# Splitting the fourth column group of P as well, its low half by a subtraction on TensorE and a ScalarE copy

## The reference, cut to what matters

```python
Wh = x @ W                                      # x: 4096 x 256 after a layer norm
e = leaky_relu(e_src[:, None] + e_dst[None, :], 0.2)
e = where((adj > 0) | eye, e, -9e15)            # adj: 4096 x 4096
alpha = softmax(e, axis=1)
x = x + alpha @ Wh                              # the attention stage
x = x + ffn(layernorm(x))                       # router, top 2 of 8 experts, two products
```

## Time and profile before

| what | value |
|---|---|
| median of three runs | 993.97 us |
| the profiled execution | 993.66 us |
| its span, from first to last instruction | 991.9 us |
| TensorE busy | 948.2 us, 96% |
| VectorE busy | 790.4 us, 80% |
| ScalarE busy | 613.7 us, 62% |
| GpSimd busy | 635.0 us, 64% |
| granted TensorE clock | 0.995 |

### The profile page before, as it was taken

One profiled execution on the slowest core, in us unless ns is written; L12 is line 12 of the kernel. 1 busy time (PEld: TensorE's weight loads), 2 busy tenths in 40 slices (PEclk: granted clock), 3 DMA queues, 4 the chain that ended last, 5 costly groups with the idle time before them and its releaser, 6 DMA issues. The chain is left out here.

```text
span 991.9 us, 22957 instructions
## 1 busy us (share of the span) xinstructions
PE 948.2 (96%) x7550; PEld 797.4 (80%) x7551; DVE 790.4 (80%) x1210; ACT 613.7 (62%) x900; POOL 635.0 (64%) x632
## 2 busy tenths in 40 slices
PE   4999999999999999999999999999999999999994
PEld 3888999889988898889888977777777777777762
DVE  7689998999999999999999446787666676577653
ACT  3789898878888887878786544334333433333441
POOL 5312251295875865847729458888888888888652
PEclk9999999999999999999999999999999999999998
DMA  8548879787888697886877986443332332232321
GB/s 276 98 160 233 294 230 273 220 234 251 249 247 294 184 296 227 251 248 196 262 252 202 360 340 205 92 111 60 60 55 44 49 58 43 43 54 42 45 34 22
DMA packets 92236, 170.97 MB, mean 172 GB/s; under 512 B 19952, under 2 KB 69360, under 8 KB 83824
## 3 DMA queue, kind: packets, MB, share of 16 engines
q1 hardware_dynamic: 58384, 134.07, 40.4%
q0 software_dynamic: 24048, 26.23, 16.9%
q10 hardware_dynamic: 9712, 9.45, 3.4%
HBM read 136.91 MB, written 41.19 MB: 180 GB/s over the span
## 5 line engine op out<-in xcount | busy, mean ns | idle before, releaser
L1130 ACT ACTIVATE hf<-tp,b_cols 128x256 f32<-128x256 f32 (+1 forms) x312 | 116.2, 459 | 177.0 <-PE tp L882 174.3
L774 PE MATMUL acc<-wh,pt_hi 128*128 128x256 f16 x768 | 209.4, 273 | 0.0
L775 PE MATMUL acc<-wh,pt_hi 128*128 128x256 f16 x768 | 209.4, 273 | 0.0
L776 PE MATMUL acc<-wh,pt_lo 128*128 128x256 f16 x768 | 209.4, 273 | 0.0
L552 POOL TENSOR_TENSOR x_late<-x_late,wsp 128x1024 f32<-128x1024 f32 x32 | 78.8, 2463 | 170.0 <-DMA x_late<-in_L_ffn_W 164.9
L898 PE MATMUL acc<-w_sb,h_hi 128*128 x568 | 171.1, 379 | 5.3 <-issue 3.9
L1279 DVE SCALAR_TENSOR_TENSOR sc<-t_row,s_col 128x2048 f32<-128x2048 f32 x64 | 162.6, 2541 | 8.6 <-PE tp L755 6.7
L658 POOL DMA_INDIRECT out<-y_sb,yidx x71 | 121.7, 1714 | 66.7 <-DVE y_sb L1602 39.6
L880 PE MATMUL tp<-x_hi,w_sb 128*128 128x256 f16 (+1 forms) x624 | 161.3, 264 | 1.9 <-ACT hf L1130 1.8
L882 PE MATMUL tp<-x_down,w_sb 128*128 128x256 f16 (+1 forms) x624 | 161.4, 264 | 0.0
L881 PE MATMUL tp<-x_lo,w_sb 128*128 128x256 f16 (+1 forms) x624 | 161.0, 263 | 0.0
(11 more groups left out here) (240 smaller groups left out, 1787.8 us busy)
## 6 DMA issues: line engine op xcount, KB each, us to landing
adj_sb<-in_adj SPq DMA_DIRECT2D x64, 1024.0 KB, 7.4
x_late<-in_L_ffn_W SPq DMA_DIRECT2D x32, 512.0 KB, 9.8
wsplit_dram<-wsp SPq DMA_DIRECT2D x32, 512.0 KB, 8.9
w_sb<-wsplit_dram SPq DMA_DIRECT2D x32, 512.0 KB, 8.9
xs<-rows_dram ACTq DMA_DIRECT2D x32, 260.0 KB, 3.4
wsp<-in_L_ffn_W POOLq DMA_DIRECT2D x32, 256.0 KB, 4.8
x<-in_x SPq DMA_DIRECT2D x32, 128.0 KB, 9.6
out<-x SPq DMA_DIRECT2D x32, 128.0 KB
```

Source lines behind the costliest of these rows:

```text
L774: pe.matmul(o, pt_hi[g][:, cols], wh[:, j, 0, :], start=(j == 0), stop=False)
L775: pe.matmul(o, pt_hi[g][:, cols], wh[:, j, 1, :], start=False, stop=False)
L776: m = pe.matmul(o, pt_lo[g][:, cols], wh[:, j, 0, :], start=False, stop=False)
```

## The change

- Group 3 is split as the others are: H3 writes f16 into `pt_hi[3]`. `wh` now holds all 32 tiles in high and low halves, so `wh32` and `pt32` are gone and A3 is 24 f16 matmuls.
- The low half of group 3 isn't made by VectorE. A new piece on TensorE, here called S (`subtract_high`), waits for H3 and adds two matmuls onto the transposed values still in `tp[1]`: the stationary operand is `minus`, an identity times -1/1024, the moving one is 512 columns of `pt_hi[3]` each. What remains in the bank is P less its high half. A new piece on ScalarE, here called R (`p_rest`), waits for S and copies the bank as f16 into `pt_lo[3]`.
- TensorE's order becomes T0, A2 of i-1, T1, A3 of i-1, T2, A0, T3, A1, S. T1 and A3 wait for R of tile i-1, S waits for H3.
- ScalarE's order becomes R of i-1, H0, first mask half, H1, exps, and so on as before.
- The transposes are written as matmuls with `is_transpose`, so that for group 3 only the first of each bank clears it.
- The four pairs that were in `wh32` get a `wh_lo` on VectorE. `wh_lo(4)` and `wh_lo(5)` come after `wh_lo(3)`; `wh_lo(10)` and `wh_lo(11)` come after `masked(1, 1)`. The waits for them grow with it, and `project(14)` now waits for `wh_lo(10)`.
- GpSimd makes `minus`, one more constant ahead of TensorE's start.

```diff
         def p_transpose(i, u, g):
                 if g == 1 and i > 0:
-                    pe.wait_ge(s_hi, G * i)
+                    pe.wait_ge(s_lq, i)
...
+            def subtract_high(i):
+                pe.wait_ge(s_hi, G * i + G)
+                for h in range(2):
+                    cols = slice(h * GW // 2, (h + 1) * GW // 2)
+                    m = pe.matmul(tp[1][:, cols], minus[:, :], pt_hi[GS][:, cols], start=False, stop=True, skip_group_check=True)
+                m.then_inc(s_sub, 1)
...
                     p_transpose(i, u, 0)
...
+                if i > 0:
+                    av(i - 1, 1 - u, 2)
+                if now:
                     p_transpose(i, u, 1)
                 if i > 0:
-                    av(i - 1, 1 - u, 2)
                     av(i - 1, 1 - u, 3)
...
                     av(i, u, 1)
+                    subtract_high(i)
...
+            def p_rest(i):
+                act.wait_ge(s_sub, i + 1)
+                if within(i, 1, T):
+                    act.wait_ge(s_av, G * i)
+                act.activation(pt_lo[GS][:, :], tp[1][:, :], ACT.Copy, scale=PSCALE).then_inc(s_lq, 1)
...
+                if i > 0:
+                    p_rest(i - 1)
                 if now:
                     p_hi(i, 0)
...
                 if ahead:
                     mask(i + 2, u, 0)
+                if now:
+                    p_hi(i, 1)
```

More of the change, by code:

```diff
@@ L123, in build @@
         sc = [sb(f"sc{u}", [P, N], F32, front) for u in range(2)]
[L124 to L128, removed]
+        wh = sb("wh", [P, T, 2, D], F16, front)
+        pt_hi = [sb(f"pt_hi{g}", [P, GW], F16, front) for g in range(G)]
+        pt_lo = [sb(f"pt_lo{g}", [P, GW], F16, front) for g in range(G)]
         x_late = sb("x_late", [P, N], F32, front)
@@ L160, in build @@
         off_diag = sb("off_diag", [P, P], BF16, front)
+        minus = sb("minus", [P, P], F16, front)
         lg = sb("lg", [P, RB, E], F32, front)
@@ L180, in build @@
         xnt_pair += [wsp[1 + p // 2][:, (p % 2) * 4 * D:(p % 2 + 1) * 4 * D].bitcast(F32) for p in range(6)]
-        xnt_pair += [b[:, :].bitcast(F32) for b in pt_hi + pt_lo]
+        xnt_pair += [b[:, :].bitcast(F32) for b in pt_hi[0:GS] + pt_lo[0:GS]]
         late_pairs = [0, 1, 2, 3, 12, 13, 10, 11, 4, 5, 14, 15, 6, 7, 8, 9]
-        lows = [p < 2 * TS // 4 for p in late_pairs]
         side = (xt_ps, rt_ps)
@@ L265, in build @@
         s_lo = sem("p_lo_done")
+        s_sub = sem("p_high_subtracted")
+        s_lq = sem("p_lo_by_act_done")
         s_av = sem("av_done")
@@ L513, in _ @@
                       allow_small_or_imprecise_dtypes=True).then_inc(s_pc, 1)
+            pool.wait_ge(s_pc, 1)
+            pool.tensor_scalar(minus[:, :], ident[:, :], -1.0 / PSCALE, 0.0, ALU.mult, ALU.add).then_inc(s_pc, 1)
             def scales(m):
@@ L687, in _ @@
         def _(pe):
-            pe.wait_ge(s_pc, 8)
+            pe.wait_ge(s_pc, 9)
             def pair_t(p):
@@ L722, in project @@
                     pe.wait_ge(s_whh, max(2, 2 * (j - 3)))
-                    pe.wait_ge(s_whl, max(2, 2 * sum(lows[:j - 3])))
+                    pe.wait_ge(s_whl, max(2, 2 * (j - 3)))
                 for h in range(2):
@@ L747, in p_transpose @@
                 if g == 1 and i > 0:
[L748 removed]
+                    pe.wait_ge(s_lq, i)
                 if g == 1 and i == 0:
[L750 removed]
+                    pe.wait_ge(s_whl, T - 2)
                     pe.wait_ge(s_whh, T - 2)
@@ L754, in p_transpose @@
                 for c in range(GJ):
-                    m = pe.transpose(tp[g % 2][:, c * P:(c + 1) * P], sc[u][:, (GJ * g + c) * P:(GJ * g + c + 1) * P], ident[:, :])
+                    m = pe.matmul(tp[g % 2][:, c * P:(c + 1) * P], sc[u][:, (GJ * g + c) * P:(GJ * g + c + 1) * P], ident[:, :],
+                                  is_transpose=True, start=(g < GS or c % (GJ // 2) == 0), stop=True, skip_group_check=True)
                 m.then_inc(s_t, 1)
@@ L763, in av @@
                 else:
-                    pe.wait_ge(s_hi, G * i + G)
+                    pe.wait_ge(s_lq, i + 1)
                 if g == 0 and within(i, 2, T):
@@ L767, in av @@
                 if g == 1 and i == 0:
-                    pe.wait_ge(s_whl, TS)
+                    pe.wait_ge(s_whl, T)
                     pe.wait_ge(s_whh, T)
@@ L772, in av @@
                     cols = slice(c * P, (c + 1) * P)
[L773 to L778, removed]
-                m.then_inc(s_av, 1)
+                    pe.matmul(o, pt_hi[g][:, cols], wh[:, j, 0, :], start=(j == 0), stop=False)
+                    pe.matmul(o, pt_hi[g][:, cols], wh[:, j, 1, :], start=False, stop=False)
+                    m = pe.matmul(o, pt_lo[g][:, cols], wh[:, j, 0, :], start=False, stop=(j == T - 1))
+                m.then_inc(s_av, 1)
+            def subtract_high(i):
[4 more added lines that the diff above has]
+                m.then_inc(s_sub, 1)
             def router_t(b, h):
@@ L837, in attend @@
                     av(i, u, 1)
+                    subtract_high(i)
                 if in_batch(b) and q == 2:
                     router_mm(b, 1)
-            pe.wait_ge(s_whl, 2 * sum(lows[:NP - 2]))
+            pe.wait_ge(s_whl, T - 4)
             pe.wait_ge(s_whh, T - 4)
@@ L959, in wh_of @@
             def wh_of(n):
-                return wh32[:, n - TS:n - TS + 2, :] if n >= TS else wh[:, n:n + 2, 0, :]
+                return wh[:, n:n + 2, 0, :]
             def wh_hi(j):
@@ L995, in p_hi @@
                     act.wait_ge(s_av, G * i + g - 3)
-                dst = pt_hi[g] if g < GS else pt32
-                act.activation(dst[:, :], tp[g % 2][:, :], ACT.Copy, scale=PSCALE).then_inc(s_hi, 1)
+                act.activation(pt_hi[g][:, :], tp[g % 2][:, :], ACT.Copy, scale=PSCALE).then_inc(s_hi, 1)
+            def p_rest(i):
[3 more added lines that the diff above has]
+                act.activation(pt_lo[GS][:, :], tp[1][:, :], ACT.Copy, scale=PSCALE).then_inc(s_lq, 1)
             def normalise(b, k):
@@ L1060, in attend @@
                 ahead = i + 2 < T
+                if i > 0:
+                    p_rest(i - 1)
                 if now:
                     p_hi(i, 0)
-                    if i == 0:
-                        wh_hi(NP - 1)
+                if i == 0:
+                    wh_hi(NP - 1)
                     p_hi(i, 1)
-                if i == 0:
                     first_step()
@@ L1106, in _ @@
                 attend(i)
+            p_rest(T - 1)
             def expert_of(t):
@@ L1474, in _ @@
             wh_lo(3)
+            wh_lo(4)
+            wh_lo(5)
             wh_lo(6)
@@ L1482, in _ @@
             masked(1, 1)
-            for j in range(12, NP - 1):
+            for j in range(10, NP - 1):
                 wh_lo(j)
```

1 line of the change is left out of this document (removed).

## The result

The changed kernel takes 1008.95 us, median of four runs (1005.1 to 1010.25), against 994.38 for the kernel before on the same chip (993.95 to 996.27): a ratio of 1.0134 [1.0101, 1.0167]. It is slower, as forecast, by 14.6 us where 9 were forecast. Its profiled execution took 1005.1 us with a span of 1003.2, 11.3 us over the span before; that is the one to hold against the sum. (In the experiments, three executions of other kernels came out one and a quarter to two and a half times as long as their neighbours; they are left out.)

A forecast was written before the change was run, and what follows sets the result against it. TensorE seemed the bound, with the new ring through ScalarE, H3 and S deciding; run-up 3.3, blocks 6.9 and tail -0.9 gave +9.3 us on 993.66, so 1003 (chance 0.70, own range 997 to 1009), given range 992 to 1011.

The forecast's parts named there:

- The plain ring: Plain tile, from one S through ScalarE and H3 to the next S: 14.71 us instead of 14.81, TensorE waiting 0.3.
- The normalising tile: Tile where ScalarE also does four normalise copies: 16.74 us instead of 14.81, TensorE waiting 2.3 for H3.
- The routing tile: Tile where TensorE also does the routers' work: 17.06 us instead of 18.20, so 1.14 less.
- The run-up: Before tile 0 and through the first tiles: T0 of tile 0 1.4 us later, T0 of tile 3 3.4 later.
- first rival: TensorE's saving comes through, each tile 0.42 us shorter: 980 us, or 987 with half the ScalarE charge regained; chance 0.13.
- The third: S runs at the f32 pace, 0.86 us instead of 0.43: 13.8 us more, 1017; chance 0.06 together with the fourth.
- the fourth: Adding onto the transposed bank needs extra instructions, looking like the third in time; chance 0.06 together with the third.
- The second: A draw at 993 us, within 0.3%: VectorE has 62 us of work in a block of 64.3; chance 0.11.
- The blocks: Groups of four tiles from tile 4 to tile 30, summed against the kernel before: +6.9 us in all.
- the one-hot tile 19: Tile where TensorE waits in `router_pos` for the one-hots, 6.39 us after L1 starts: 16.4 us against 16.47.
- The tail: From T0 of tile 31 to the expert stage: two shorter A3, less one S and 0.3 of waiting, -0.9 us.
- VectorE has 8% left.: Attention stage: VectorE busy 469.3 of 511.9 us, read as 8% left, with TensorE at 501.0 seeming the bound.

The follow-up runs named there:

- T1 in the middle of A2: The changed kernel with T1 moved between the two halves of A2 on TensorE: 1004.41 us, ratio 1.0083.
- S twice: The changed kernel with the subtraction made in two passes of half the weight, four matmuls instead of two, same result: 1022.12 us, ratio 1.0272.
- the changed kernel's copy: The changed kernel run again unedited, beside three later experiments: 1006.16 us, ratio 1.0124.
- T1 in the middle and the copies spread: The changed kernel with T1 between the halves of A2 and four normalise copies spread over normalising and routing tiles: 996.95 us, ratio 1.0015.

## Why the prediction was right, and where its sizes were off

Right, by its steps (predicted, then measured in the profiled execution):

- A3 2.62 and 2.62; S 0.43 and 0.43 to 0.45; TensorE's own work in a plain tile 14.39 and 14.40 (T1 in the middle of A2).
- The plain ring 14.71 and 14.71 to 14.72, with a wait of 0.3 ahead of S. By the issue gap of the Trainium skill ("TensorE: Matmul & The Clock Gate", Back-to-back issue gap) S would have been 0.26 (and this ring 14.54, not below 14.5 as the prediction has it); S twice added 0.43 to it, so the row it was taken from held.
- The normalising tile 16.74 and 16.67 to 17.4, with the wait of 2.3 for H3 at 2.1 to 2.3; VectorE's L2 waits 1.55 there (over 1.4 was said). The routing tile 17.06 and 16.93 to 17.28, but for the two with a fallen clock (18.6).
- R: 0.92 from its start to the next copy's (337.06 to 337.98) and 1.02 long, not 1.15. The Trainium skill ("ScalarE: Activation LUTs", What ACT_TABLE_LOAD costs) has a second figure, 186 ns plus 0.833 ns per element for an ACTIVATE with immediate scale and bias, and 93 ns of overlap in a row. From it I estimate 1.04 and 0.95. That is the one to use for R, whose scale is an immediate, and the rows agree with it within 0.03; the figure that the prediction took is given there for a bias that is a pointer operand, which R hasn't.
- The run-up: T0 of tile 0 1.1 us later (1.4 was said), T0 of tile 3 3.2 (3.4). T1 of tile 1 waits 1.60 for R. In the profile of the changed kernel's copy the two are 2.4 and 4.5 later, so this part varies by over 1 us from one execution to the next.

Of the first rival (TensorE's saving comes through, 980) little is left: with T1 in the middle and the copies spread, the kernel still isn't faster than before. The third (S at the f32 pace) and the fourth are answered by S's 0.44 us. The second, a draw, is where the kernel goes once the ring is mended. It came true of that kernel, not of this one.

Off were three sizes:

1. *The missing term is TensorE's clock.* The prediction took the clock as full throughout, as the earlier trace rows show it. With the added waits came stretches of 3.4 us at 1.2 GHz, 1.7 us each. The profiled execution has two, both behind waits of over 2 us: 3.3 of its 11.3 us. That the waits bring them is argued from all the profiles, not shown by a run of its own. Its mean clock is 0.994, that of the other three runs 0.991 to 0.992, and these are 3 to 5 us longer; this is most of why the median is 1009 and not 1005. That each further loss is such a stretch was seen only in profiled executions, not in those three.
2. *The blocks.* Without the clock they gave +5.8 where 6.9 was said (T0 to T0: tiles 4 to 7 +1.2 for 2.2, then +2.5, +0.6, +1.3, +0.7, -0.7, +0.2 for 0.6, 1.5, 0.6, 1.4, 0.7, -0.1). Single blocks miss by up to 1.9, in both directions; two of the causes were traced, both on VectorE. In tile 9 its masked starts 1.75 us after T0, not 0.8 as in tile 17, so the exps start later and the tile has 17.43. In the one-hot tile 19 the step from L1 (376.12) to the one-hots (383.39) is 7.27 instead of 6.39, 0.9 more, and the tile 17.26 instead of 16.4: one instruction on the way takes 1.97 us where it took 1.15 before, and 0.15 where GpSimd leaves it alone, as the rows at the end show. The tail gave -0.7 for -0.9. So 3.1 + 5.8 + 3.3 - 0.7 = 11.5 at the end of the stage's products, and 11.3 in the span.
3. *"VectorE has 8% left."* True over the stage, and misleading. Within a block VectorE works 61.9 us of 64.3, and its rests sit where it waits for others (1.36 us for H2 in tile 17, behind the same four normalise copies). With half of A3 left out the block didn't get shorter. Nor are the 61.9 all work: in tiles 16 to 19 of the kernel before some 3.8 us of them, an estimate, are VectorE held up beside GpSimd (two scores halves of 4.32 and 3.18 instead of 2.34, and 1.15 instead of 0.15; see the end). The second rival had this reason (62 us of work in a block of 64.3); the first rival's 980 took for granted that TensorE's savings are worth their length. They weren't, and it should have had less than 0.13.

Open: whether the change pays if VectorE is relieved first, for instance with S and R for a second group in place of its L, or with GpSimd's `TENSOR_TENSOR` of L553 moved out of its way; neither was tried.

## What to carry to other kernels

When work moves to an engine with a small share, follow its order round the ring to the next tile: here 0.92 us on an engine at 62% cost nothing by itself, while one wait moved ahead of the bound's whole next tile cost 2 us every fourth tile. A saving on the busiest engine is worth at most the distance to the second busiest within the same block, and here it was worth nothing there; measure this first by leaving some of the work out. An engine's busy time can hold time in which another engine holds it up, so compare the lengths of equal instructions before taking it for work. Where waits of about 2 us are new on TensorE, allow for the clock as well, and move the work that causes them rather than the work that shows them: spreading four small copies gave back more than any change to the new pieces.

## What the runs showed of the hardware that was not expected

- In an otherwise full stage TensorE's granted clock fell to 1.2 GHz for 3.4 us (once 6.8) around the end of waits of 1.69 to 3.57 us, 27 times in the attention stages of eleven profiles, and nowhere else in them. It didn't fall behind all of them: two of the seven waits of 2.1 to 2.3 us for H3 in the changed kernel's profile. In the one profile with these waits filled with useless matmuls it didn't fall in the attention.
- The way from ScalarE through S and back, the end of H3 (353.03) to the start of R (353.73), is 0.70 us, of which 0.61 is S itself: by this trace the two handovers between these engines cost less than 0.1 us together. The ends of matmuls are modelled, so the split is rough; the 0.70 isn't.
- VectorE and GpSimd hold each other up. Some VectorE instructions take longer beside GpSimd's `TENSOR_TENSOR` of L553. The timeline of VectorE in the changed kernel, tiles 7 and 17 to 19, then that of GpSimd:

```profile
186.26 0.15 DVE L1380 TENSOR_TENSOR gap_l<-top 128x4 f32<-128x4 f32 x1
...
344.35 2.34 DVE L1298 SCALAR_TENSOR_TENSOR sc<-t_row,s_col 128x2048 f32<-128x2048 f32 x1
...
350.46 4.12 DVE L1298 SCALAR_TENSOR_TENSOR sc<-t_row,s_col 128x2048 f32<-128x2048 f32 x1
...
361.57 2.34 DVE L1298 SCALAR_TENSOR_TENSOR sc<-t_row,s_col 128x2048 f32<-128x2048 f32 x1
...
380.73 1.97 DVE L1380 TENSOR_TENSOR gap_l<-top 128x4 f32<-128x4 f32 x1
```

```profile
350.28 2.15 POOL L553 TENSOR_TENSOR x_late<-x_late,wsp 128x1024 f32<-128x1024 f32 x1
...
363.41 2.50 POOL L553 TENSOR_TENSOR x_late<-x_late,wsp 128x1024 f32<-128x1024 f32 x1 [3.26 <-DMA x_late<-in_L_ffn_W]
...
380.56 2.12 POOL L553 TENSOR_TENSOR x_late<-x_late,wsp 128x1024 f32<-128x1024 f32 x1 [10.57 <-DMA x_late<-in_L_ffn_W]
```

A scores half by itself has 2.34 us (344.35). The one at 350.46 begins 0.18 us after GpSimd's instruction and has 4.12. The one at 361.57 is under way when GpSimd's begins; it keeps its 2.34, and GpSimd's takes 2.50 instead of some 2.13. The instruction of 128 x 4 has 0.15 us by itself (186.26); the one at 380.73 lasts until 382.70, 0.02 us longer than GpSimd's.

The eleven profiles repeat this. Of their 704 scores halves 111 took over 2.45 us, all of them beside that `TENSOR_TENSOR`; in 87 GpSimd's had begun first, in 23 more it began less than 0.2 us later. Where it began later than that beside a half of usual length, GpSimd's took up to 4.1 us, longer by about what was left of the half. L0 to L2, which read one operand from PSUM, took at most 1.23 us in all of the 251 that ran beside it. So for the scores halves the one that begins second waits for the other; masked is held up by 2.6 us though its row begins 0.55 us ahead. None of this was tried by itself, but rows this regular leave little room for chance. The Trainium skill ("GPSIMD Engine Reference", 1. Specifications) lists contention between the two engines for VectorE instructions with two SBUF inputs, which the scores and the 128 x 4 instruction are; the trace agrees.
